# Second feed-forward stage of a macaron block: statistics taken in the attention loop, routing begun a chunk sooner, two more shared pairs behind the routed work

## The reference

```
x = x + 0.5 * ffn(layernorm(x))        # FFN1
x = x + ssd(layernorm(x))              # attention stage
x = x + 0.5 * ffn(layernorm(x))        # FFN2, same weights

ffn(x): sc = sigmoid(x @ router.T) + bias        # 16 experts in 4 groups of 4
        two best groups, four best experts in them, weights scaled to 2.5
        routed = sum over 4 experts of w * down(silu(gate(x)) * up(x))
        shared = an MLP that every token takes
ssd(x): x, z, B, C = x @ in_proj.T ; x = silu(conv(x))
        h = h*exp(-exp(A)) + B*x ; y = C*h       # scan over the sequence
        layernorm(y * silu(z)) @ out_proj.T
```

## Time and profile before

| | us |
|---|---|
| median of 3 runs | 1429.34 (1428.12 to 1429.48) |
| the profiled execution | 1430.07 |
| its span in the trace | 1428.3 |
| PE, DVE, ACT, POOL busy in the span | 1268.3, 896.4, 628.5, 972.8 |

### The profile page before, as it was taken

The page is one execution under the profiler, slowest core; times in us unless marked ns, Lnnn a source line. Parts: engine busy times, 40 slices in busy tenths (PEclk is TensorE's granted clock), DMA queues, the critical chain, the costliest instruction groups (busy, mean ns, idle before and its releaser), DMA issues.

```text
span 1428.3 us, 23451 instructions
## 1 busy us (share of the span) xinstructions
PE 1268.3 (89%) x6920; PEld 1095.2 (77%) x6920; DVE 896.4 (63%) x2190; ACT 628.5 (44%) x1092; POOL 972.8 (68%) x1348
## 2 busy tenths in 40 slices
PE   5793999999996789999999999977699999999990
PEld 5593888888885568888888888866588888888880
DVE  5764722254657987878778786866685622354553
ACT  2143334434434456666565566553243334434420
POOL 3578882284876687978879797831588881484866
PEclk9796999999998899999999999998899999999995
DMA  9975565587754200010000000111355566687653
GB/s 350 408 292 170 198 242 185 198 266 240 264 190 167 77 31 16 31 46 16 31 16 30 15 30 30 61 52 45 141 203 192 198 231 214 217 274 244 224 171 114
DMA packets 86921, 218.44 MB, mean 153 GB/s; under 512 B 16272, under 2 KB 28560, under 8 KB 85904
## 3 DMA queue, kind: packets, MB, share of 16 engines
q1 hardware_dynamic: 62224, 149.82, 29.4%
q0 software_dynamic: 24576, 67.14, 14.7%
HBM read 109.43 MB, written 107.48 MB: 152 GB/s over the span
## 4 chain that ended last, share of the span: by engine, by line
PE 46%; DVE 17%; POOL 16%; issue 14%; DMA 4%; ACT 2%; POOLq 0%; DVEq 0%; SPq 0%; ACTq 0%; another core or an unknown queue 0%
PE ps L1116 12%; POOL f_gbuf L516 7%; PE ps L1150 6%; POOL xg L490 5%; PE ps L1082 4%; PE ps L2101 4%; DVE at_xs L1898 4%; PE ps L2103 3%; PE ps L2102 3%; PE ps L1121 3%; PE ps L2162 2%; DMA f_gbuf<-yg,f_rows 2%; PE ps L1132 1%; PE ps L2187 1%; PE ps L2151 1%
## 5 line engine op out<-in xcount | busy, mean ns | idle before, releaser
L516 POOL DMA_INDIRECT f_gbuf<-yg,f_rows x256 | 266.5, 1041 | 190.5 <-DMA yg<-f_yo 136.7
L490 POOL DMA_INDIRECT xg<-f_xn,f_rows x256 | 252.3, 986 | 88.7 <-issue 55.7
L1116 PE MATMUL ps<-f_wgu,f_xT 128*128 x1248 | 296.6, 381 | 0.0
L1116 PEld LDWEIGHTS ps<-f_wgu,f_xT 128*128 128x128 f32 x1248 | 225.7, 191 | 24.9 <-issue 0.3
L858 DVE TENSOR_TENSOR f_h<-ps,f_sg 128x256 f32<-128x256 f32 x156 | 66.0, 423 | 228.1 <-ACT f_sg L573 227.5
L573 ACT ACTIVATE f_sg<-ps 128x256 f32<-128x256 f32 x156 | 59.8, 383 | 316.7 <-PE ps L1116 314.8
L890 DVE SCALAR_TENSOR_TENSOR f_xin<-f_gbuf,f_w,f_xin 128x256 f32<-128x256 f32 x256 | 128.1, 500 | 80.8 <-DMA f_gbuf<-yg,f_rows 73.7
L1150 PE MATMUL ps<-f_wd,f_hT 128*128 x624 | 161.5, 381 | 7.2 <-DVE f_hT L866 7.2
L1898 DVE SCALAR_TENSOR_TENSOR at_xs<-at_raw,at_taps,at_xs 128x512 f32<-128x512 f32 x136 | 135.6, 999 | 6.5 <-POOL at_xs L1548 3.8
L560 ACT COPY f_xT<-ps 128x512 f32<-128x512 f32 x216 | 125.5, 581 | 32.1 <-PE ps L1082 23.2
L1121 PE MATMUL ps<-f_xT,f_wgu_sh 128*128 128x256 f32 x512 | 128.2, 401 | 11.7 <-DVE f_hT L862 11.7
(11 more groups left out here) (261 smaller groups left out, 2713.9 us busy)
## 6 DMA issues: line engine op xcount, KB each, us to landing
f_xq<-xg SPq DMA_DIRECT2D x78, 512.0 KB, 4.8
yg<-f_yo SPq DMA_DIRECT2D x156, 256.0 KB, 2.8
xg<-f_gbuf SPq DMA_DIRECT2D x39, 512.0 KB, 6.7
f_wgu<-in_gate_up SPq DMA_DIRECT2D x4, 1280.0 KB, 13.2
f_xin<-in_x SPq DMA_DIRECT2D x8, 512.0 KB, 7.4
xg<-f_xn,f_rows POOLq DMA_INDIRECT x256
f_gbuf<-yg,f_rows POOLq DMA_INDIRECT x256, 3.7
x<-f_xin SPq DMA_DIRECT2D x8, 512.0 KB, 3.3
```

Of the source, the lines that this page charges most:

```text
L490: G.indirect_dma_start(xg[0:USED[g] * P, :], bass.IndirectOffsetOnAxis(ap=rows[g][:, b, k:k + 1], axis=0), xn[:, SUB * TILE0[g] + b, :], N ...
L516: G.indirect_dma_start(gbuf[:, n % GBUF, k, :], None, yg[0:USED[g] * P, :], bass.IndirectOffsetOnAxis(ap=rows[g][:, b, k:k + 1], axis=0), ...
L1116: last = T.matmul(gu_ps[:, j % 2, s * 2 * P:(s + 1) * 2 * P], x_of(k, s, d), weight(wgu[:, :, d, :], experts[s]), start=(d == 0), stop=(d ...
```

## The change

It has five parts.

1. **Statistics in the loop.** DVE takes `bn_stats` of each output chunk 0 to 27 in the attention loop, right after the residual sum (`statistics_out`). `statistics` of FFN2 keeps only `bn_aggr` for tiles 0 to 6; tile 7 is taken as before. To fit this, FFN2 loads and stores its tiles with 128 consecutive tokens a sub-tile ("(t s p)"), so that a partition's 4 KB consists of four pieces of 1 KB.
2. **FFN2's first parts earlier.** The first DVE part stands in chunk 24 (t = 6, q = 0) and no longer at the end of t = 6; statistics of tiles 0 to 6 are spread over chunks 24 to 28. The first POOL part stands at the end of POOL's chunk 24, one chunk sooner, and has five constants to set; `f_sign` follows later.
3. **Routing of group 0 a chunk sooner.** Pieces 0 to 2 stand ahead of `at_X_lo` of chunk 30, counts and pieces 5 and 6 ahead of `at_X_lo` of chunk 31. PE counts after `project_out(29)`. POOL takes the roots of FFN2 in three batches, and only that of tile 7 between scatters.
4. **First scatter ahead of the last root** on POOL.
5. **Order of FFN2.** Shared pairs 8 and 9 move behind the routed work of group 0 (where 10 and 11 were) and 10 and 11 to the end, where now six pairs stand; eight pairs, before ten, stand ahead of the routed work. Counts and pieces of group 1 come one shared step sooner.

```diff
         yield from each("route", 14, 15)
-        yield from each("shared", 7, 8, 9)
+        yield from each("shared", 7)
...
-            yield from each("shared", *((5, 10) if fresh else (10, 11)))
-    if fresh:
-        yield from each("shared", 11)
+            yield from each("shared", *((5, 10) if fresh else (8, 9)))
+    yield from each("shared", *((11,) if fresh else (10, 11)))
     yield from each("shared", 12, 13, 14, 15)
...
-        pool.wait_ge(init_done, 7 + fresh)
+        pool.wait_ge(init_done, 8 if fresh else 5)
...
-                if not fresh and g == 0 and b in (1, 2, 4, 5):
-                    rstd_of({1: 4, 2: 5, 4: 6, 5: 7}[b])
+                if not fresh and g == 0 and b == 6:
+                    rstd_of_tiles(7, 8)
...
+                dve.wait_ge(attn["stats_taken"], SUB * (t + 1))
+                of = attn["bn_out"][:, SUB * t:SUB * (t + 1), :]
...
-        dve.wait_ge(init_done, 7 + fresh)
-        dve.wait_ge(small_in, 32)
+        dve.wait_ge(init_done, 8 if fresh else 5)
...
+        def statistics_out(c, q):
+            dve.wait_ge(s["out_added"], c + 1)
+            at = bass.ds(c, 1) if not isinstance(c, int) else slice(c, c + 1)
+            V.bn_stats(bn_out[:, at, :].rearrange("p o n -> p (o n)"), x_res[:, q, :]).then_inc(s["stats_taken"], 1)
...
+                    if q == 0 and not start:
+                        statistics_out(c - 1, SUB - 1)
+                    if q > 0 and more(t, 1):
+                        statistics_out(c - 1, q - 1)
+                    if not more(t, 1):
+                        next(after_it, None)
+                    if q < SUB - 1 and isinstance(t, int) and t == NT - 2:
+                        next(after_it, None)
                     if q == 1 and more(t, 1):
                         rest_of_g(t + 1, nx)
                     if q == 2 and more(t, 2):
                         normalize(t + 2)
                     rest_of_X(c + 1)
...
-                if q == 1 and isinstance(t, int) and t == NT - 2:
+                if q < SUB - 1 and isinstance(t, int) and t == NT - 2:
                     next(after_it, None)
```

More of the change, by code:

```diff
@@ L111, in ffn_events @@
         yield from each("shared", 1)
[L112 to L115, removed]
+        yield from each("route", 8, 9, 10, 11)
+        yield from each("shared", 2, 3, 4, 5)
         yield from each("route", 12, 13)
@@ L821, in name_tiles @@
             new_chain()
+            if g == 0 and not fresh:
+                dve.wait_ge(init_done, 7)
             if g:
@@ L997, in vector @@
             statistics(1)
-            yield
             statistics(2)
             yield
-            for i in range(3):
+            statistics(3)
+            statistics(4)
+            yield
+            statistics(5)
+            yield
+            statistics(6)
+            yield
+            dve.wait_ge(small_in, 32)
+            for i in range(2):
                 route_piece(0, i)
-                yield
+            route_piece(0, 2)
+            yield
             copy_counts(0, START)
@@ L1009, in vector @@
             route_piece(0, 6)
-            yield
-            statistics(3)
-            yield
-            statistics(4)
             yield
@@ L1597, in tile @@
                     first_tap(t + 1, nx, 2 * q + 1)
-                if not more(t, 1) and q == 0:
-                    next(after_it, None)
                 if q in (0, 2) or q == SUB - 1 and not more(t, 1) and not final(c):
@@ L2076, in tile @@
                     rest_of_X(c + 1)
-                    if q == 1 and not more(t, 1):
-                        next(after_it, None)
                 else:
@@ L2084, in tile @@
                     add_out(t, c - 1, q - 1)
+                    if not more(t, 1):
+                        settle(dve)
                     statistics_y(c)
@@ L2282, in tile @@
                     last.then_inc(s["y_in_psum"], 1)
-                if not more(t, 1) and q == 0:
+                if not more(t, 1) and q < 2:
                     settle(pe)
@@ L2295, in tile @@
                     project_out(c - 1)
-                if not more(t, 1) and q < 2:
+                if not more(t, 1) and q < 3:
                     settle(pe)
@@ L2312, in tile @@
                     project_z(c + 1, par, q + 1, 0)
-                    if not more(t, 1) and q < 2:
+                    if not more(t, 1) and q == 0:
                         settle(pe)
@@ L2329, in tile @@
                     project_x(t + 2, par, 1, "xT_lo_ready", t + 3)
-                if not more(t, 1) and q < 2:
+                if not more(t, 1) and q == 0:
+                    next(after_it, None)
+                if isinstance(t, int) and t == NT - 2 and q == SUB - 1:
+                    settle(pe)
+                    pe.wait_ge(s["raw_ready"], CT * NT)
                     next(after_it, None)
```

120 lines of the change are left out of this document (62 added, 58 removed).

## The result

The changed kernel takes 1435.4 us (median of 7 runs, 1432.85 to 1437.34) against 1429.34 (now also 7 runs, 1427.81 to 1432.05). The ratio on record is 1.0033, 95% interval 1.0018 to 1.0049; the two medians alone make 1.0042. It is slower, where I had forecast 1423.5 in a range of 1411 to 1434.

What follows compares the result with a forecast made beforehand. Two chains, POOL's scatters and PE's FFN2 steps, were taken to set the routed work's start and so the end. −20.0 + 3.0 + 11.2 + 0 = −5.8 on 1430.07 gave 1424.3, median forecast 1423.5, range 1411 to 1434.

Steps and rivals of the forecast that it cites:

- The stall in chunk 24: DVE's first FFN2 part waits 10.5 us for POOL's five constants ahead of chunk 25's `at_X_lo`; charged 11.2 us.
- The cost in the loop: In the attention loop, `bn_stats` ahead of `at_X_lo` costs 0.43 us in 7 q = 1 chunks; charged 3.0 us.
- where DVE waits for ACT before `at_X_lo` there is room: In the attention loop, five of 21 chunks have 8.0 us of DVE waiting, so `bn_stats` there was charged nothing.
- My slower rival: Third rival: `bn_stats` between `add_out` and `at_X_lo` costs 0.6 us in 28 chunks, 17 us; total 1437, chance 0.14.
- The gain on PE's chain: From the last attention chunk through FFN2's steps, PE reaches routed work 20.2 us sooner; routed work was forecast 20 sooner.
- with the root 1.8 sooner: In chunk 31, POOL's root starts at 1002.3 instead of 1004.10, helping finish `at_ynT_lo` near 1008.3 instead of 1016.7.
- chunk 30 comes some 3 us sooner: Late in the attention stage, chunk 30 gains some 3 us because tile statistics and PE's steps leave its way.
- the charge for group 1's pieces: In FFN2, counts and pieces stand one shared pair closer to their inputs; 1.5 us of new PE waiting charged.
- The gain on POOL's chain: Scatters before the routed work: earlier counts and fewer roots between scatters end them about 1061.0 against 1083.7, 22.7 us sooner.
- The end: After routed work, 41.7 us of gathers cover six shared pairs' 33.9 us on PE; nothing charged.
- The sentence on the Trainium skill's rule: By the busiest-engine-first rule, 12 us on DVE at 63% beside PE at 89% would be free, the sum 3.0 lower.
- The second rival: Pieces and counts delay chunks 30 and 31 by 5 or 6 us more; scatters gain only 14 to 15; 1429, chance 0.2.

Runs made afterwards that it cites:

- The last experiment: Counts and pieces of group 1 one shared pair later, against the changed kernel with its wait late and `bn_stats` behind `at_X_lo`: 1413.69 us, ratio 0.9877 to the kernel before.

## Why the prediction was wrong

- **The stall in chunk 24** was right in place, cause and size: a DVE wait of 10.5 forecast and 10.50 seen, and moving the wait gave 7 us of the total back (9.0 of the 10.7 in the trace). One slip stands in its sum: 11.2 less the wait of 2.40 is 8.8 and not 9.2, so the charge should have been 10.8 and not 11.2. From chunk 24 to 28, 10.7 were measured.
- **The cost in the loop** failed: 2.6 forecast to chunk 24, 6.8 measured. The failing step was "where DVE waits for ACT before `at_X_lo` there is room". I priced `bn_stats` by its own 0.43 and asked only where DVE waits. I did not ask what the instruction behind it would then run against. The q = 1 places cost 1.9, near the forecast; the rest is the place in q = 2, where the normalization behind `bn_stats` runs against POOL's second long instruction as well. My slower rival had the right place and the wrong price: `bn_stats` is not on every chunk's path, and behind the cast it costs 0.1 in the whole loop.
- **The gain on PE's chain** failed, and it is the largest part of the miss: 20 forecast, 9.9 measured (8.1 on PE's chain, and the 1.75 that PE had waited for the rows before). The start of FFN2 on PE was put 10.4 sooner and came 2.7 sooner. The step was "with the root 1.8 sooner", and ahead of it "chunk 30 comes some 3 us sooner": it took the statistics out of the way of the last chunks and did not count the pieces and counts that now stand ahead of the casts of chunks 30 and 31. Against chunk 28 these casts came 4.4 and 4.0 later, and the root 3.5 later. From the cast of chunk 31 to the root there were 12.0 us, before 12.6, so the loss lies ahead of that cast; the slow output matmuls (4.43, before 2.49) and the 1.99 that DVE's residual sum of chunk 30 waited for PE (before 1.64) only took up what was saved there. Behind the root the sum left 3.4 us for projecting out, from 1008.3 to 1011.7, where the earlier trace rows show 5.4 (1016.78 to 1022.15); it took 5.3. Its terms for the cast make 1008.6 and not 1008.3.
  In FFN2's own stretch 9.8 was forecast (11.3 for two pairs, less 1.5) and 5.4 measured. The pairs were priced too high: with them alone moved, PE's work there fell by 9.9 (65.2 to 55.3). Ahead of the sorted rows PE has 32 L1121 matmuls fewer, which is two pairs, but only 8 of L1150, which is one. Then the charge for group 1's pieces was too low: the wait was 2.60, another 1.01 (before, 0.88 in all), and L1170 behind it took 3.5 us to the next start and not 1.73. The last experiment gave this back (59.1 to 55.2). For the later start no run did: with the casts ahead of the pieces, the wait moved to the other casts. What would bring that time back stays open.
- **The gain on POOL's chain** was also smaller (first scatter 17.0 sooner, 19.4 forecast; the last ended 16.9 sooner, 22.7 forecast), but in the changed kernel that no longer bound anything. That the two chains bind together before the change is confirmed from both sides.
- **The end** was right: the gathers cover six shared pairs. The stretch was 1.5 shorter, not longer.
- **The sentence on the Trainium skill's rule** ("Perfetto Trace Analysis", Identifying the Most-Contended Engine) stood on the right side: spare share on DVE did not by itself make the work free. The place decided it, and no count of instructions: 6.8 us ahead of the cast, 0.1 behind it.

The second rival (the tail gains less) and part of the third came true together, and I had priced them one at a time. With the forecast's stall they make the slower kernel. Two of the signs that I had named for being wrong were seen: 6.8 us over the loop's six tiles are over 1 us each, and the first `f_xq` transpose came 9.9 and not 20 us closer to chunk 28.

## What to carry to other kernels

When an instruction goes into an in-order queue, price also what stands behind it: on what other engine's work does that now fall, and which of its instructions share a path to memory. A wait added early in a woven program is worth its place only if something there needs it; here what the wait in chunk 24 guarded was first needed over 80 us later. Where two chains end together, an edit on one shows nothing by itself, and a gain counted on both must be counted with each one's own new waits.

## What the runs showed of the hardware

Some DVE instructions are much slower beside POOL's elementwise work. With the wait moved, the small `tensor_scalar` instructions of the statistics ran while POOL scaled `at_g`, and each ended 0.03 us behind the POOL instruction that it met (the POOL rows are from narrower windows, one instruction each):

```profile
889.49 0.43 DVE L1940 BATCH_NORM_STATS2 at_bn_out<-at_x_res 128x6 f32<-128x256 f32 x1
890.76 0.94 DVE L691 TENSOR_SCALAR f_nbias<-f_mv 128x4 f32<-128x4 f32 x1
891.61 1.33 DVE L692 TENSOR_SCALAR f_var<-f_mv 128x4 f32<-128x4 f32 x1
...
890.39 1.27 POOL L1549 TENSOR_TENSOR at_g<-at_bc,at_tab 128x512 f32<-128x512 f32 x1
891.63 1.29 POOL L1549 TENSOR_TENSOR at_g<-at_bc,at_tab 128x512 f32<-128x512 f32 x1
```

The same two instructions took 0.17 and 0.16 in the changed kernel (902.34 and 902.42), where POOL's next long instruction began only at 902.52. The Trainium skill describes this on the page "SBUF — State Buffer", Who interferes with whom: DVE and GpSimd share one pair of ports under an exclusive lock, `tensor_scalar` is among the operations that can take it when its operands meet certain conditions, and the one that comes second is blocked until the first is done. The first of these rows (0.94) agrees with that, the other cases only in part. `f_var` (1.33) and the fourth normalizing instruction (1.47) ended just behind POOL's instruction, but they began 0.02 us ahead of it, and the second normalizing instruction took its 0.40 (668.33) wholly within POOL's L1569. So the runs show that DVE can be held up until POOL is done, and do not show by what order it is decided. `bn_stats` showed no such effect: it took 0.43 here inside POOL's work on `at_g`.
